# A Flamingo block on one core: both heads' probabilities turned back to back, two turned banks, values product in a work bank

## The reference

```
x = x + tanh(g_xattn[0]) * _L0_xattn_ref(ctx, _layernorm(x), mask, ...)   # stage one
x = x + tanh(g_ffn[0])   * _L0_ffn_ref(_layernorm(x), ...)                # router in stage one, experts after it
x = x + tanh(g_xattn[1]) * _L1_xattn_ref(_layernorm(x), ctx, ctx, ...)
x = x + tanh(g_ffn[1])   * _L1_ffn_ref(_layernorm(x), ...)
```

```
q = ln(latents) @ w_q                      # latents: the standardised x, 256 rows
kv = concat([ln(ctx), ln(latents)]) @ w_kv # 376 rows, k and v of 8 heads of 64
sim = q k^T / 8, masked;  attn = softmax(sim);  out = attn v
return ln(out @ w_out)
probs = softmax(x @ Wr + br)               # 8 experts, two chosen, at most 40 rows an expert and batch
```

## Time and profile before

| | |
|---|---|
| median of three runs | 2334.22 us (2328.33 to 2338.77) |
| the profiled execution, its own time | 2332.35 us |
| its span | 2330.2 us |
| PE busy in the span | 2229.5 us, 96% |
| DVE, ACT, POOL busy | 1767.9, 1287.4, 659.9 us |
| stage one | about the first 1190 us |

### The profile page before, as it was taken

One profiled execution on the slowest core, in us unless ns is written; L12 is line 12 of the kernel. 1 busy time (PEld: TensorE's weight loads), 2 busy tenths in 40 slices (PEclk: granted clock), 3 DMA queues, 4 the chain that ended last, 5 costly groups with the idle time before them and its releaser, 6 DMA issues. The chain is left out here.

```text
span 2330.2 us, 52907 instructions
## 1 busy us (share of the span) xinstructions
PE 2229.5 (96%) x15232; PEld 1867.0 (80%) x15232; DVE 1767.9 (76%) x6078; ACT 1287.4 (55%) x3250; POOL 659.9 (28%) x1162
## 2 busy tenths in 40 slices
PE   6999999999999999999899999999899999999998
PEld 5777777777677777777699999999788888888887
DVE  5888878788777887788865555555588888888897
ACT  5776666666666766667543333333354444454444
POOL 1123222232232322322210000001355555555542
PEclk9999999999999999999999999999999999999999
DMA  6220010110100100001042222222122111221110
GB/s 212 87 92 29 27 38 26 29 36 19 37 27 28 37 26 29 30 27 32 15 142 77 81 83 83 82 64 74 55 57 61 54 57 51 60 60 60 58 44 19
DMA packets 111557, 128.34 MB, mean 55 GB/s; under 512 B 14898, under 2 KB 98089, under 8 KB 111264
## 3 DMA queue, kind: packets, MB, share of 16 engines
q1 hardware_dynamic: 98249, 105.06, 14.2%
q0 software_dynamic: 12288, 21.21, 3.2%
q10 hardware_dynamic: 855, 0.19, 0.1%
HBM read 84.26 MB, written 54.53 MB: 60 GB/s over the span
## 5 line engine op out<-in xcount | busy, mean ns | idle before, releaser
L709 ACT ACTIVATE a_prob<-a_prob,a_nmax 128x376 f32<-128x376 f32 x512 | 307.1, 604 | 26.8 <-DVE a_nmax L855 26.0
L1116 PEld LDWEIGHTS a_turned<-keep_ident,a_prob 128*128 128x128 f32 (+1 forms) x1536 | 173.6, 139 | 160.0 <-issue 118.0
L1116 PE MATMUL a_turned<-keep_ident,a_prob 128*128 128x128 f32 (+1 forms) x1536 | 265.1, 281 | 31.3 <-DVE a_probT L874 27.1
L1420 ACT ACTIVATE e_hidden<-e_first,keep_b 128x256 f32<-128x256 f32 x320 | 134.4, 472 | 286.8 <-PE e_first L80 285.4
L855 DVE CUSTOM_DVE_ANT_0 a_prob<-a_score,a_mask_row 128x376 f32<-128x376 f32 x512 | 262.5, 541 | 19.9 <-DVE r_lg L257 9.7
L717 ACT ACTIVATE a_probT<-a_turned 128x384 f32<-128x384 f32 x256 | 125.9, 492 | 241.9 <-PE a_turned L1116 236.4
L80 PE MATMUL e_second<-e_w,e_hidden 128*128 128x256 f32 x1920 | 239.5, 284 | 0.0
L80 PEld LDWEIGHTS e_second<-e_w,e_hidden 128*128 128x128 f32 x1920 | 232.6, 192 | 0.0
L874 DVE COPY a_probT<-a_turned 128x384 f32<-128x384 f32 x256 | 141.3, 552 | 119.4 <-PE a_turned L1116 61.2
L171 POOL TENSOR_SCALAR r_var<-r_mv 128x2 f32<-128x2 f32 x64 | 12.3, 192 | 686.1 <-DVE r_mv L889 520.7
L867 DVE TENSOR_SCALAR a_prob<-a_prob,a_rden 128x376 f32<-128x376 f32 x512 | 201.3, 419 | 2.2
(11 more groups left out here) (212 smaller groups left out, 5114.6 us busy)
## 6 DMA issues: line engine op xcount, KB each, us to landing
w_in<-W SPq DMA_DIRECT2D x32, 512.0 KB
slots<-a_zeros SPq DMA_DIRECT2D x8, 1280.0 KB, 9.1
keep_rows<-slots SPq DMA_DIRECT2D x40, 256.0 KB, 3.8
answers<-e_y SPq DMA_DIRECT2D x40, 256.0 KB, 2.2
a_xn<-x SPq DMA_DIRECT2D x32, 256.0 KB, 3.6
a_xr<-x SPq DMA_DIRECT2D x32, 256.0 KB, 2.8
x<-r_x SPq DMA_DIRECT2D x32, 256.0 KB, 2.7
w_in<-x SPq DMA_DIRECT2D x32, 256.0 KB, 2.8
```

Source lines behind the costliest of these rows:

```text
L709: nc.scalar.activation(prob[:, u % 4, a], prob[:, u % 4, a], ACT.Exp, bias=nmax[:, u % 4, a:a + 1], scale=-1.0, accum_out=den[:, u % 4, a: ...
L1116: last = nc.tensor.transpose(turned[0:hi - lo, j * P:(j + 1) * P], prob[:, u % 4, a, lo:hi], ident[:])
L1420: nc.scalar.activation(hidden[:, 2 * j + i], first[:, j, i * CH:(i + 1) * CH], ACT.Relu, bias=b1[:, 2 * j + i, bass.ds(e, 1)]).then_inc(re ...
```

## The change

PSUM is dealt out anew, in stage one:

```
-        turned = pb("a_turned", [P, 512])
-        work = [pb(f"a_work{i}", [P, 512]) for i in range(2)]
+        turned = [pb(f"a_turned{i}", [P, 512]) for i in range(2)]
+        work = [pb("a_work0", [P, 512]), values]
```

Each head has its turned bank. `work[1]` is now the bank `values` itself: Q, two parts of V, the output, the turned context and the router share it. The values product moves to `work[0]`, beside K, one part of V and `turn_x`. `turn_prob` turns both heads at once:

```
-            def turn_prob(b, u, a):
-
-                eng.wait_ge(norm_ok[a], NG * b + u + 1)
-                at_least(eng, prob_ok[1 - a], NG * b + u + a)
-                for j, lo, hi in VALUE_ROWS:
...
-                last.then_inc(turned_ok[a], 1)
+            def turn_prob(b, u):
+
+                for a in range(2):
+                    eng.wait_ge(norm_ok[a], NG * b + u + 1)
+                    at_least(eng, prob_ok[a], NG * b + u)
+                for a in range(2):
+                    for j, lo, hi in VALUE_ROWS:
...
+                    last.then_inc(turned_ok[a], 1)
```

The waits that guard the banks follow. Those that the prediction speaks of:

```
             def turn_x(b):
                 eng.wait_ge(xh_ok, 3 * (b + 1))
-                at_least(eng, k_hi, KI * (b - 1) + 3)
+                if isinstance(b, int) and b == 1:
+                    eng.wait_ge(k_hi, 3)
+                at_least(eng, att_lo, KI * (b - 2) + 3)
...
             def turn_c(b):
                 eng.wait_ge(xh_ok, 3 * (b + 1))
-                at_least(eng, att_lo, KI * (b - 2) + 3)
+                at_least(eng, v_ok, 3 * (b - 1) + 1)
+                at_least(eng, soft, N_SOFT * (b - 3) + 1)
...
             def times_v(b, p, m):
                 for a in range(2):
                     eng.wait_ge(prob_ok[a], NG * b + 2 * m + 2)
                 if m == 0:
                     eng.wait_ge(v_ok, 3 * (b + 1))
-                    at_least(eng, route, N_ROUTE * (b - 2) + 1)
...
-                elif m == 1:
-                    eng.wait_ge(att_lo, KI * b + 1)
...
+                elif isinstance(b, int) and b == B - 1:
+                    eng.wait_ge(att_lo, KI * b + m)
                 else:
-                    eng.wait_ge(att_lo, KI * b + 3)
...
+                    eng.wait_ge(k_hi, KI * (b + 1) + m + 1)
```

```
-                    turn_prob(s - 2, 6, 1)
-                    times_v(s - 2, p, 2)
+                    turn_prob(s - 2, 6)
```

More of the change, by code:

```diff
@@ L341, in router_logits @@
         eng.wait_ge(rT_out, b + 1)
+        if not (isinstance(b, int) and b >= B - 2):
+            eng.wait_ge(v_ok, 3 * (b + 2) + 1)
         for i in range(QT):
@@ L476, in attend @@
         LAST = 3
-        turned_keys = turned[:, 0:3 * P].rearrange("p (j q) -> p j q", j=3)
+        turned_keys = [bank[:, 0:3 * P].rearrange("p (j q) -> p j q", j=3) for bank in turned]
         def live(b, last=B):
@@ L670, in affine_c @@
                 for k in range(KD):
-                    nc.scalar.activation(kvin[:, k, 0:C], values[:, k * C:(k + 1) * C], ACT.Identity,
+                    nc.scalar.activation(kvin[:, k, 0:C], work[1][:, k * C:(k + 1) * C], ACT.Identity,
                                          bias=aff[:, 3, k:k + 1], scale=aff[:, 2, k:k + 1]).then_inc(kvc_ok, 1)
@@ L722, in att_high @@
                 at_least(eng, out_ok, b)
-                nc.scalar.activation(att2[:, 0, m], values[:, 0:S], ACT.Copy).then_inc(att_hi, 1)
+                nc.scalar.activation(att2[:, 0, m], work[0][:, 0:S], ACT.Copy).then_inc(att_hi, 1)
             def w1_higher(n):
@@ L905, in weights_lower @@
                     .then_inc(w_low, 1)
-            nc.vector.memset(turned[:], 0.0).then_inc(const_ok, 1)
+            for bank in turned:
+                nc.vector.memset(bank[:], 0.0).then_inc(const_ok, 1)
             nc.vector.memset(mask_row[:, :, C:NKV], 0.0).then_inc(const_ok, 1)
@@ L925, in step @@
                     weights_lower(3, wo[:], stage_o)
-                if live(s - 1):
-                    mask_line(s - 1, q)
                 if live(s - 2):
-                    normalise(s - 2, 2, 1)
+                    normalise(s - 2, 0, 0)
+                if live(s - 3):
+                    turned_out(s - 3, 7, 1)
+                if live(s):
+                    stat(s, p)
+                if live(s - 2):
+                    row_max(s - 2, p, 2, 0)
+                    row_max(s - 2, p, 2, 1)
+                    over_sum(s - 2, 1)
+                    row_max(s - 2, p, 3, 1)
+                if live(s - 1) and not (isinstance(s, int) and s == 1):
+                    kvin_low(s - 1, q, 0)
+                if live(s - 2):
+                    row_max(s - 2, p, 3, 0)
+                    normalise(s - 2, 1, 0)
+                    normalise(s - 2, 1, 1)
+                    over_sum(s - 2, 2)
+                    turned_out(s - 2, 0, 1)
                 if live(s - 3):
@@ L1046, in turn_c @@
                 eng.wait_ge(xh_ok, 3 * (b + 1))
-                at_least(eng, att_lo, KI * (b - 2) + 3)
+                at_least(eng, v_ok, 3 * (b - 1) + 1)
+                at_least(eng, soft, N_SOFT * (b - 3) + 1)
                 for k in range(KD):
-                    last = nc.tensor.transpose(values[:, k * C:(k + 1) * C],
+                    last = nc.tensor.transpose(work[1][:, k * C:(k + 1) * C],
                                                xh[0:C, 2, k * P:(k + 1) * P], ident[0:C, 0:C])
```

318 lines of the change are left out of this document (143 added, 175 removed).

## The result

The changed kernel takes 2353.09 us (median of four runs, 2350.57 to 2354.29), the kernel before beside it 2335.24 us (2328.33 to 2338.77): 1.0079 times as long, interval 1.0054 to 1.0104. The forecast was 2330 us, "no change, just"; the time lies in the range, but the change is a loss of 0.8%, and the side was wrong. The profiled execution took 2354.29 us, with a span of 2352.4 us.

A forecast was written before the change was run, and what follows sets the result against it. PE's queue plus its waits was taken to bound stage one; -1.0 -0.9 -1.48 +3.1 = -0.3 us a pair, -4 us over 15 pairs, gave 2330 us. Range for 8 in 10: 2294 to 2358 us; the forecast's own 2314 to 2344.

The forecast's parts named there:

- Waits at the loop's end: PE's 0.94 and 0.54 us waits behind DVE's loop-end stop go, -1.48 us a pair; 1.5 us of new waits counted nil.
- rival 2: DVE's loop-end stop lands on PE at scores or unit 1's turn: +36 us, 2370 us, half of it 2352; chance 0.20.
- Fill and drain: Pipeline's filling and draining outside the loop: pieces kept, only moved over a step's border, costing nothing.
- The shared work bank: turn_x, near a step's end, waits for att_low of pair 2, seen late beside POOL's DMAs: +3.1 us a pair.
- Order on PE: Joined heads leave three fewer ways into f32 products in each stage-one step: 0.5 us saved a step, -1.0 a pair.
- The second step's turn: PE's wait before the turn behind the router in a pair's second step goes: -0.9 us a pair.
- the wait at the output product: PE's 0.94 us wait before the output product in a pair's first step, behind DVE's loop-end stop, goes.
- Rival 3: DVE's normalisations shut POOL out during the indirect DMAs, ending them 1.6 us later a step: 2375 us; chance 0.05.

The follow-up runs named there:

- DVE's half of the unit 7 edit: Changed kernel with only DVE's order edited: row maxima of unit 2 ahead of the copy of unit 7 and the batch statistics; ratio 1.0037 to the kernel before.
- unit 7 edit: Changed kernel with unit 7's turn behind the scores of units 2 and 3 on PE, its DVE copy behind unit 2's row maxima; 2300.91 us, ratio 0.9979.
- the statistics alone: Changed kernel with only the batch statistics moved behind the row maxima of unit 2, the copy of unit 7 staying first; ratio 1.0038 to the kernel before.

## Why the prediction was wrong, point by point

- *"Waits at the loop's end ... -1.48 and nothing new."* This is the first step that failed. The prediction laid out DVE's queue, found 1.5 us, and then set it to nothing because `turn_x` would have held PE before. Measured: the waits at the head of a pass are 1.6 to 1.9 us, and a loop's end costs about 2.1 us in either order, so nothing of the 1.48 us was won. On top of it TensorE's clock falls behind 3 of the 11 loop ends of after (6 on the other kind of chip, none in one execution of the same loop), 1.6 us each, a term that the prediction didn't have at all. DVE's half of the unit 7 edit and the statistics alone take 0.4 to 0.5% of time away. The mechanism was written down as rival 2, with a chance of 0.20. That its half says 2352 us, 1 us from the measured time, is luck: it put +18 us into the passes, where 10.0 were lost, and nothing into fill and drain, where 14 were.
- *"Fill and drain ... nothing."* The second step that failed: 5.6 and 8.4 us. The pieces are the same, but moving them over the border put the splits of w_out and of w1 directly ahead of a row maximum and a copy. Moving them away gave 6.3 us in the new order and nothing in the old one. About 5 of the 8.4 us are products at the lower clock; that isn't the change's alone, since two edited kernels in the old order have them too (118.3 us from batch 30 to the experts without the DMAs and 113.5 with the splits moved, against 109.3 in before). How much of the two stretches is the order's doing is open.
- *"The shared work bank ... +3.1."* Right in kind, wrong in size and in its part. The prediction had `turn_x` at B+4.8 undisturbed and at B+6.8 with the late completion, B being POOL's first DMA. It starts at B+4.9 where completions aren't late (594.00 less 589.08 us) and at B+5.4 where they are (676.71 less 671.35 us). The completion is seen 2.51 us after the product's start, not 1.56: one late, and `turn_x` is 0.5 us late, not 1.55; `turn_c` and the turn of unit 7 are late as much again, which the prediction had only for unit 7 and only small. Together 0.9 to 1.0 us a step. But it is no part of the difference: the ratio is 1.0079 where completions are late and 1.0090 where they are not, and the old order loses as much (0.8% against 0.9%).
- *"Order on PE ... -1.0."* Wrong, and it is not in the product: values product to scores is 1.45 us (621.43 to 622.88), as from values product to turn before. An undisturbed step takes 34.2 us against 34.07 before, 0.15 more, where 0.5 less was forecast: +0.3 a pair. With the unit 7 edit, which takes unit 7's turn away from behind `turn_c` and ahead of f32 scores, the step takes 33.87 us (585.12 less 551.25, `turn_x` to `turn_x`). So joining the heads saves 0.2 us a step at best.
- *"The second step's turn ... -0.9"* went as said; so did the wait at the output product.
- *Rival 3* found nothing. POOL's four DMAs of a step take 1.07, 0.98, 0.97 and 0.97 us in after; normalisations stand beside the first three and not beside the fourth. So the 0.1 us that the prediction read off as the price of a normalisation is the first DMA's own. Its sum was off as well: 31 steps of 1.6 us are 50, not 45. The rule of the Trainium skill, "SBUF — State Buffer", section "SBUF: two separate sides", that a VectorE operation in a two-port mode locks GpSimd out, shows in none of these rows; whether a normalisation runs in such a mode no run here shows.
- *The range.* 2353 us lies inside the 2294 to 2358, but that was width and not insight: the forecast's own range ended at 2344, and it was drawn narrower than its terms, whose bounds over 31 steps (order 0 to 0.7 us, `turn_x` 0.9 to 2.0) reach from about 2304 to 2359.

## What to carry to other kernels

Where a pipelined loop is rotated, ask of each engine's queue what stands directly behind its stop at the loop's end and directly behind each one-off piece in the steps outside the loop; work that PE waits for belongs first, work for the next step second, and as far back as it fills a gap of its own, not farther. A wait that two terms share must not be cancelled by one of them: the 1.5 us found at the loop's end were dropped because another wait, which is itself uncertain, might cover them. And a loss seen in the trace of before belongs to the difference only if the change removes it. A stretch at the lower clock that comes in one execution and not in the next is counted over several traces before it is charged to the change.

## What was not expected of the hardware

- Completions of PE beside POOL's indirect DMAs are seen late on two of the four chips used and not on the other two, for the same kernel at the same phase: 2.51 against 1.56 us. Without the DMAs the kernel before is 0.8% faster on a chip of the first kind. Its median moves from 2332 to 2307 us between the chips, and some 8 of these 25 us lie behind stage one; what makes the chips differ isn't known.
- At the end of a hardware loop DVE stands for 2.6 to 3.0 us, at each of the 11 loop ends of before and of after; with a body twice as long it stands 2.6 to 3.2 us, no longer to speak of, but PE now stands too, 3.3 us in the rows above. The Trainium skill, "Advanced Engine Details and Errata", section "Control Flow Timing", has a branch at about 0.05 or 0.1 us; the measured stop is far from that, so it isn't the branch alone.
- TensorE's clock fell to its lower level behind the two waits of 0.5 and 1.3 us at the head of a pass, in some passes and not in others whose rows read alike, and behind none in another execution of the same loop; why in some is open. The kernel before waits as long in all behind the same stop and had no fall in the loop in any of its three traces with two steps in the body.
